# A two-layer graph network: part of the second layer's scatter as rounded part and rest, and the last stage by groups of blocks

## The reference

```
# layer 0
e      = leaky_relu(concat(x[src], x[dst]) @ w) @ a
att    = exp(e) / segment_sum(exp(e), src)[src]
x      = layernorm(x + segment_sum(x[src] * att, dst))
# layer 1, 4 heads of 32 channels
H      = x @ W
s      = leaky_relu(H_s[src] + H_t[dst])          # H_s, H_t: two scores per head and node
s      = exp(s - max(s))
alpha  = s / (segment_sum(s, src) + 1e-8)
agg    = segment_sum(alpha * H[dst], src) + x @ residual_projection
x      = layernorm(x + elu(agg))
```

## Time and profile before

| | |
|---|---|
| the profiled execution's own time | 3574.67 us |
| its span, first to last instruction | 3572.9 us |
| TensorE busy | 3143.2 us, 88% |
| VectorE busy | 3083.1 us, 86% |
| ScalarE busy | 2138.4 us, 60% |
| GpSimd busy | 47.3 us, 1% |
| second layer's scatter, L1243 | 4802 records, first at 2397.6, last at 3473.6 us |
| `exponent`, L1268, mean of 49 | 459 ns |
| last stage, first operation to the end of the span | 3479.4 to 3572.9 us |

### The profile page before, as it was taken

The page is one execution under the profiler, slowest core; times in us unless marked ns, Lnnn a source line. Parts: engine busy times, 40 slices in busy tenths (PEclk is TensorE's granted clock), DMA queues, the critical chain, the costliest instruction groups (busy, mean ns, idle before and its releaser), DMA issues. The chain is left out here.

```text
span 3572.9 us, 97665 instructions
## 1 busy us (share of the span) xinstructions
PE 3143.2 (88%) x40120; PEld 2920.0 (82%) x40120; DVE 3083.1 (86%) x4702; ACT 2138.4 (60%) x4348; POOL 47.3 (1%) x104
## 2 busy tenths in 40 slices
PE   2666669999999999599999999969999999999980
PEld 1666657777777777599999999969999999999980
DVE  5999988899999999899999999968888888888867
ACT  1333338777787777599999999943333333333330
POOL 0000000000000000000000000000000000000000
PEclk9888879999999999799999999989999999999995
DMA  2000012222222222133333333224444444444421
GB/s 54 13 10 12 8 34 87 86 90 86 89 82 91 86 85 81 47 96 97 97 96 97 97 97 97 85 96 149 146 146 147 150 147 149 147 146 149 148 69 36
DMA packets 172961, 332.80 MB, mean 93 GB/s; under 512 B 54673, under 2 KB 108517, under 8 KB 172514
## 3 DMA queue, kind: packets, MB, share of 16 engines
q1 hardware_dynamic: 172514, 326.50, 29.7%
HBM read 320.77 MB, written 5.66 MB: 91 GB/s over the span
## 5 line engine op out<-in xcount | busy, mean ns | idle before, releaser
L1243 PE MATMUL l_acc<-e,l_lane_wide 128*128 128x132 f32 x4802 | 615.2, 280 | 0.0
L1243 PEld LDWEIGHTS l_acc<-e,l_lane_wide 128*128 128x128 f32 x4802 | 566.4, 190 | 0.0
L902 PE MATMUL l_gathered<-xp,l_src_onehot 128*128 128x128 bf16 x7203 | 463.3, 220 | 28.2 <-DVE l_src_onehot L829 28.2
L621 PE MATMUL sc_z<-sc_onehot,pq 128*128 128x256 f32 (+1 forms) x2450 | 427.1, 297 | 43.9 <-DVE sc_leaky L564 42.2
L1174 DVE TENSOR_TENSOR e<-l_gathered,l_weight 128x896 f32<-128x896 f32 x343 | 373.4, 1089 | 102.6 <-PE l_gathered L1230 102.2
L1230 PE MATMUL l_gathered<-hp,l_onehot 128*128 128x128 bf16 x7203 | 458.9, 219 | 0.0
L902 PEld LDWEIGHTS l_gathered<-xp,l_src_onehot 128*128 128x128 bf16 x7203 | 404.8, 98 | 42.8 <-DVE l_src_onehot L829 28.3
L748 DVE TENSOR_TENSOR l_lane<-iota_b,l_lane_pairs 128x896 bf16<-128x896 bf16 x686 | 421.5, 614 | 0.0
L564 DVE SCALAR_TENSOR_TENSOR sc_leaky<-sc_z,sc_leaky 128x1024 f32<-128x1024 f32 (+3 forms) x325 | 369.8, 1138 | 46.0 <-ACT sc_leaky L704 42.8
L1230 PEld LDWEIGHTS l_gathered<-hp,l_onehot 128*128 128x128 bf16 x7203 | 407.3, 98 | 0.1
L704 ACT ACTIVATE sc_leaky<-sc_z 128x1024 f32<-128x1024 f32 (+3 forms) x325 | 309.9, 953 | 154.4 <-PE sc_z L625 95.9
(11 more groups left out here) (208 smaller groups left out, 4944.9 us busy)
## 6 DMA issues: line engine op xcount, KB each, us to landing
l_got<-edge_rows_wide SPq DMA_DIRECT2D x343, 448.0 KB, 3.6
l_got<-edge_rows_src SPq DMA_DIRECT2D x343, 224.0 KB, 3.2
placed<-edge_rows SPq DMA_DIRECT2D x144, 512.0 KB, 3.6
out_dram<-X SPq DMA_DIRECT2D x1, 3072.0 KB
edge_rows<-bin_bytes SPq DMA_DIRECT2D x98, 6.1 KB
edge_rows_wide<-bin_rows SPq DMA_DIRECT2D x98, 12.2 KB
placed<-edge_rows SPq DMA_DIRECT2D x24, 64.0 KB, 2.8
placed<-edge_rows SPq DMA_DIRECT2D x6, 256.0 KB, 3.5
```

What stands on the lines that cost most here:

```text
L621: nc.tensor.matmul(z[:, b, 0:nw, :], PQ[:, b0 + b, q, 0:C], hot[:, r % HOTS, b, 0, 0:nw, :], start=(b == u and q == 0), stop=False)
L902: ins = nc.tensor.matmul(gps[:, t % 2, i * P:(i + 1) * P], hot[:, t % RING, i, :], parts[:, g * GX + i, q, :], start=(q == 0), stop=(q == 2))
L1243: ins = nc.tensor.matmul(acc[:, b % 2, 0:CW], lane_wide[:, t % 2, i, :], msg[:, t % 2, i, :], start=(n == 0), stop=(n == NB - 1))
```

## The change

In `layer1` three of the seven bins (`SPLIT` = 3) are scattered as a rounded part and a rest, side by side in one fp32r matmul of 2 x 132 columns; the rests gather in columns 132 to 263 of the accumulator. The other four go as f32 as before. VectorE weighs six bins, and the seventh is weighed by ScalarE in four activations of 32 channels, one for each head, after its rounding of the three. VectorE's `take_low` is the last of its step; on ScalarE `take_high(t)` and `weigh_last(t)` come first and `exponent`, `copy_weights(t + 1)`, `widen(t + 1)` and `take` behind them. ScalarE's `take` copies the low sums too, and GpSimd adds them to `S` and `den4` and takes one from X (for the ELU).

```
-                        pe.wait_ge(s["messages"], t - 1)
+                        pe.wait_ge(s["last_message"], t - 1)
...
-                    for i in range(GX):
-                        n = g * GX + i
-                        ins = nc.tensor.matmul(acc[:, b % 2, 0:CW], lane_wide[:, t % 2, i, :], msg[:, t % 2, i, :], start=(n == 0),
-                                               stop=(n == NB - 1))
+                    for i in range(SPLIT, GX):
+                        if i == GX - 1:
+                            pe.wait_ge(s["last_message"], t + 1)
+                        nc.tensor.matmul(acc[:, b % 2, 0:CW], lane_wide[:, t % 2, i, :].bitcast(F32), msg[:, t % 2, i, :],
+                                         start=(g == 0 and i == SPLIT), stop=False, skip_group_check=True)
+                    pe.wait_ge(s["low"], t + 1)
+                    for i in range(SPLIT):
+                        last = g == PER - 1 and i == SPLIT - 1
+                        ins = nc.tensor.matmul(acc[:, b % 2, 0:2 * CW], lane_wide[:, t % 2, i, :],
+                                               halves[:, t % 2, i].rearrange("p h c -> p (h c)"), start=False, stop=last,
+                                               skip_group_check=True)
...
+                def take_low(t):
+                    dve.wait_ge(s["high"], t + 1)
+                    nc.vector.tensor_tensor(halves[:, t % 2, :, 1, :], msg[:, t % 2, 0:SPLIT, :], halves[:, t % 2, :, 0, :],
+                                            ALU.subtract).then_inc(s["low"], 1)
...
+                def add_low(b):
+                    pool.wait_ge(s["taken"], b + 1)
+                    nc.gpsimd.tensor_tensor(S[:, b, :], S[:, b, :], lows[:, b % 2, 0:C], ALU.add)
+                    nc.gpsimd.tensor_tensor(den4[:, b, :], den4[:, b, :], lows[:, b % 2, C:CW], ALU.add).then_inc(s["summed"], 1)
...
+                def take_high(t):
+                    act.wait_ge(s["messages"], t + 1)
+                    act.wait_ge(s["weights"], t + 1)
+                    nc.scalar.copy(halves[:, t % 2, :, 0, :], msg[:, t % 2, 0:SPLIT, :]).then_inc(s["high"], 1)
+
+                def weigh_last(t):
+                    b, g = divmod(t, PER)
+                    i, n = GX - 1, g * GX + GX - 1
+                    for e in range(HEADS):
+                        ins = nc.scalar.activation(msg[:, t % 2, i, e * D:(e + 1) * D], gps[:, t % 2, i * P + e * D:i * P + (e + 1) * D],
+                                                   ACT.Copy, scale=weight[:, b % 2, n, e:e + 1])
+                    ins.then_inc(s["last_message"], 1)
```

```
+                def measure(g):
+                    dve.wait_ge(s["added"], g + 1)
+                    for i in range(count(g)):
+                        ins = nc.vector.bn_stats(stats[:, g * PER + i, :], total[:, g % BANKS, i * C:(i + 1) * C])
...
+                for c in (slice(0, 2 * PER), slice(2 * PER, NB)):
+                    ch.link(nc.vector.reciprocal(den4[:, c, :], den4[:, c, :]))
+                    for g in range(c.start // PER, -(-c.stop // PER)):
+                        divide(g)
+                        if g >= 1:
+                            add_residual(g - 1)
+                add_residual(G - 1)
+                for j in range(len(BATCHES)):
+                    for g in range(*BATCHES[j]):
+                        measure(g)
+                        if j >= 1 and g == BATCHES[j][0]:
+                            factors(j - 1)
+                    variance(j)
+                factors(len(BATCHES) - 1)
...
+                def begin(g):
+                    if g >= BANKS:
+                        wait_normed(pe, g - BANKS)
+                    nc.tensor.matmul(total[:, g % BANKS, 0:count(g) * C], k.ident[:], flat(X, g), start=True, stop=False)
+                def add_up(g):
+                    pe.wait_ge(s["positive"], g + 1)
+                    nc.tensor.matmul(total[:, g % BANKS, 0:count(g) * C], k.ident[:], flat(S, g), start=False, stop=False)
+                    pe.wait_ge(s["exponent"], g + 1)
+                    nc.tensor.matmul(total[:, g % BANKS, 0:count(g) * C], k.ident[:], flat(R, g), start=False, stop=True
+                                     ).then_inc(s["added"], 1)
+                for g in range(BANKS):
+                    begin(g)
+                for g in range(G):
+                    add_up(g)
+                    if BANKS <= g + 4 < G:
+                        begin(g + 4)
...
+                for g in range(G + 1):
+                    if g < G:
+                        negative(g)
+                    if g >= 1:
+                        positive(g - 1)
+                        exponent(g - 1)
+                for j in range(len(BATCHES)):
+                    act.wait_ge(s["variance"], j + 1)
+                    nc.scalar.activation(dev[:, batch(j)], squares[:, batch(j)], ACT.Sqrt, scale=1.0 / C, bias=ln_eps[:]
+                                         ).then_inc(s["deviation"], 1)
+                    act.wait_ge(s["factors"], j + 1)
+                    for g in range(*BATCHES[j]):
+                        if g not in BY_VECTOR:
+                            norm(g)
```

More of the change, by code:

```diff
@@ L1103, in layer1 @@
             "chain", "const", "hot", "scored", "read", "top", "all", "negated", "exp", "staged", "lane", "lane_wide", "gathered",
-            "messages", "weights", "added", "taken")}
+            "messages", "last_message", "weights", "high", "low", "added", "taken", "summed")}
         loaded = [ctx.semaphore(f"l1_loaded{h}") for h in range(LOADS)]
@@ L1291, in _ @@
                         stage((t + 4) // PER)
+                    if 0 <= t < R:
+                        take_high(t)
+                        weigh_last(t)
                     if (t + 1) % PER == 0 and 0 <= (t + 1) // PER < NB:
@@ L1917, in _, with add_and_norm @@
                 nc.vector.tensor_tensor(xs[:], X[:], rden[:].unsqueeze(2).to_broadcast([P, NB, C]), ALU.mult)
-def add_and_norm(nc, k, tag, X, S, R, before, out):
+def add_and_norm(nc, k, tag, X, S):
     NB = k.NI
@@ L1925, in add_and_norm @@
         ask = ctx.enter_context(nc.sbuf_tensor(f"{tag}_ask", [P, 1], F32))
-        chain, a_req, a_done, fin, st = (ctx.semaphore(f"{tag}_{n}") for n in (
-            "chain", "act_asked", "act_done", "finished", "stored"))
+        chain, a_req, a_done = (ctx.semaphore(f"{tag}_{n}") for n in (
+            "chain", "act_asked", "act_done"))
         asked = []
@@ L1956, in _, with lower_by_one, elu_and_norm, sb @@
                     emit().then_inc(a_done, 1)
+def lower_by_one(nc, X):
+    with Stage(nc):
+        with nc.Block() as block:
+            @block.vector
+            def _(dve):
+                nc.vector.tensor_scalar(X[:, 0:NBK, :], X[:, 0:NBK, :], -1.0, None, ALU.add)
+def elu_and_norm(nc, k, X, S, R, den4, eps, out):
+    NB, PER, BANKS, N = NBK, 4, 8, out.shape[0]
+    G = -(-NB // PER)
+    BATCHES = ((0, 2), (2, 5), (5, 8), (8, 11), (11, G))
+    BY_VECTOR = (3, 7, 11)
+    with Stage(nc) as ctx:
+        def sb(name, shape, dt=F32):
+            return ctx.enter_context(nc.sbuf_tensor(f"fin_{name}", shape, dt))
+        s = {n: ctx.semaphore("fin_" + n) for n in (
+            "chain", "gap", "decay", "divided", "summed", "negative", "positive", "exponent", "added", "stats", "variance",
+            "deviation", "factors", "normed_act", "normed_dve", "stored")}
+        stats = sb("stats", [P, NB, 6])
+        twice, apart, squares = sb("twice_mean", [P, NB]), sb("apart", [P, NB]), sb("squares", [P, NB])
+        dev, rstd, shift, ln_eps = sb("deviation", [P, NB]), sb("rstd", [P, NB]), sb("shift", [P, NB]), sb("ln_eps", [P, 1])
+        total = ctx.enter_context(nc.psum_tensor("fin_total", [P, BANKS, 512], F32))
+        def blocks(g):
+            return slice(g * PER, min((g + 1) * PER, NB))
+        def count(g):
+            return min(PER, NB - g * PER)
+        def flat(t, g):
+            return t[:, blocks(g), :].rearrange("p b c -> p (b c)")
+        def batch(j):
+            return slice(BATCHES[j][0] * PER, min(BATCHES[j][1] * PER, NB))
+        def wait_normed(eng, g):
+            if g in BY_VECTOR:
+                eng.wait_ge(s["normed_dve"], len([i for i in BY_VECTOR if i <= g]))
+            else:
+                eng.wait_ge(s["normed_act"], g + 1 - len([i for i in BY_VECTOR if i <= g]))
+        with nc.Block() as block:
@@ L1958, in _ @@
             @block.sync
             def _(sp):
[L1960 to L1966, removed]
+                for g in range(G):
+                    wait_normed(sp, g)
+                    rows = slice(g * PER * P, min((g * PER + count(g)) * P, N))
+                    if count(g) * P == rows.stop - rows.start:
+                        sp.dma_start(out[rows].rearrange("(b p) c -> p b c", p=P), X[:, blocks(g), :]).then_inc(s["stored"], 16)
+                    else:
+                        sp.dma_start(out[rows], X[0:rows.stop - rows.start, g * PER, :]).then_inc(s["stored"], 16)
@@ new lines, in _ @@
```

(8 more changed lines are left out.)

112 lines of the change are left out of this document (84 added, 28 removed).

## The result

Four runs of the changed kernel gave a median of 3476.99 us (3475.55 to 3479.29), four of the kernel before 3575.99. The ratio is 0.9724, interval 0.9707 to 0.9741: faster by 99 us, 3480 was forecast. The profiled execution took 3477.6, its span 3475.8.

The account below looks back on a forecast made before the run. TensorE bounded layer 1's loop, VectorE much of the last stage. Gains 59.5 + 2.7 - 1.2 + 35 = 96.0 from 3574.7 gave 3478.7; with the median 1.7 above, 3480 (60%, 3465 to 3495; 8 in 10, 3448 to 3512).

Parts of the forecast that it names:

- 59.5 + 2.7 - 1.2 + 35 = 96.0: Gains in us: layer 1's 334 steps, its last nine steps, minus GpSimd's bare additions at the end, plus the last stage.
- TensorE's step, 2.86: Layer 1: eight f32 records 0.93 and three fp32r ones 0.40 cut TensorE's step by 0.30 to 2.86 us.
- VectorE's step, 2.65 and 2.02: Layer 1: VectorE needs 2.65 us a step, find_top 2.02 more each seventh: 20.64 in seven steps, 2.95 a step.
- The stall, 0.84 in seven steps: Layer 1: TensorE waits for the last message in the step with find_top, making the step 2.98 us.
- rivals B and D: Layer 1: B, late last message, 3.07 a step, 3510, 15%; D, ScalarE's order sets the step, 3.31, 3594, 3%.
- Rival A: Layer 1: VectorE's lateness is absorbed and TensorE alone sets 2.86 a step; 3440, 8%.
- GpSimd beside VectorE: Layer 1: GpSimd pays for contention, 452 ns alone and 597 beside VectorE; VectorE's two-input subtraction kept to 0.69 us.
- Rival E: Layer 1: VectorE stands still while GpSimd works, 61 us on it, of which 50 come through; 3530, 2%.
- The last stage: From 93.5 to 58.5 us, gain 35; TensorE idles behind group 0's norm, which stands behind all ScalarE passes.
- The lower clock: Last stage: after its pause TensorE starts at clock 0.51 for its first 4 us of work, costing 1.75 us.
- ScalarE's twelve norms: Last stage's tail: twelve norms at 0.26 take 3.2 us, with the last batch's root behind them.
- Rival C: Last stage: TensorE stays at 1.2 GHz all through, 15 us more; 3495, 12%.

Follow-up runs that it names:

- last message last: The changed kernel with the seventh bin's matmul moved behind the three fp32r ones in layer 1's scatter: 3468.7 us, ratio 0.9716, step 2.945 us.
- GpSimd free: The changed kernel without GpSimd's addition of the low sums and the one taken from X: 3477.2 us, ratio 0.9724, step 2.972 us.
- after: The changed kernel itself, against the kernel before: 3477.0 us, ratio 0.9724, layer 1 step 2.973 us.
- the later scatter and make before the rest: The changed kernel with scatter one step later on TensorE, three buffers, and VectorE's make ahead of its rest: 3435.8 us, ratio 0.9619, step 2.859 us.
- four bins split: The changed kernel with four of seven bins split instead of three (SPLIT = 4): 3538.8 us, ratio 0.9906, step 3.158 us.

## Why the prediction was right

**The frame.** The sum was 59.5 + 2.7 - 1.2 + 35 = 96.0 from the profiled execution. Alone, layer 1 gave 62.4, where 59.5 + 2.7 - 1.2 = 61.0 were forecast, and the last stage 33.0 where it was 35. The two misses have opposite signs. That the profiled execution came within 1.1 us of the forecast for it (3477.6 against 3478.7) is luck; the terms are good to 1 or 2 us.

**TensorE's step, 2.86.** Measured 2.86. The two terms were off against each other: the f32 records 0.88 instead of 0.93, the three fp32r ones 0.45 instead of 0.40. That was a matter of reading: by their starts has the six f32 records at 0.64 and the four fp32r ones at 0.56, where the prediction gave them 0.68 and 0.52. The 264 columns cost like the 256: records start 0.12 us apart behind a first distance of 0.20, in layer 0 as here. No figure is near the upper bound of 0.233.

**VectorE's step, 2.65 and 2.02.** Measured 2.62 to 2.67 and 2.02. The subtraction took 0.57 and the four activations 0.82, as worked out, which rules out rivals B and D.

**The stall, 0.84 in seven steps.** Measured 0.76, at the place named: the last message, in the step with `find_top`. The step is TensorE's 2.86 and this stall; VectorE's sum lies just below it, at 2.945 where it sets the pace (last message last). The two limits are thus only 0.03 a step apart, some 9 us in all. By the sum alone (2.95) the forecast would have been 3470, inside the range as well, so the total could not have told them apart. The runs do. GpSimd free changed nothing because VectorE is late by the same 2.0 us at each `find_top` as long as it is back on time before it. With the scatter's order changed the step fell with VectorE's work unchanged, but only down to its sum. My expectations for both runs took the sum for the limit in after, against the prediction's own working; the first failed, and the second named the right number with a wrong reason. Rival A (TensorE alone) appears only when both limits are gone, in the kernel with the later scatter and make before the rest.

**GpSimd beside VectorE.** The prediction held that GpSimd alone pays. That was wrong: VectorE's subtraction lengthened from 570 to 687 ns when GpSimd worked beside it (the 48 of 343 that overlap one of GpSimd's additions took 683 to 687, the others 556 to 574), which is what the Trainium skill, GPSIMD Engine Reference, Specifications, says of instructions with two SBUF inputs. It cost nothing, as it fell where VectorE had time (the kernel with GpSimd free). GpSimd paid too: its 128-element addition took 454 ns alone and up to 762 beside VectorE. The evidence in the earlier trace rows did not bear on the question: in the kernel before, 48 of the 49 additions of L890 overlap VectorE's weighing and `make`, and none a subtraction. Rival E was out all the same, as the kernel with GpSimd free shows.

**The last stage.** Counted from 3415.7, the first operation's place if it had stood directly ahead of the second: ScalarE's passes ended at 25.0 (25.6 forecast), TensorE stood from 16.2 to 28.7 (17 to 28.8), took up work at clock 0.50 for some 6 us (4), ended at 48.2 (47.5), the last store went at 55.9 (54), the end came at 60.1 (58.5). Three terms were mis-sized. The lower clock cost more: the first four f32 matmuls of 512 columns took 1.87, 1.71, 1.71 and 1.27 us from start to start, 3.1 us above four times 0.86, where 1.75 had been put in. The columns cost less: 0.86 for 512 is 1.68 ns a column instead of 1.76, 0.8 us less for 9600. ScalarE's twelve norms took 4.13 us until the root behind them (3464.80 to 3468.93), 0.345 apart, instead of 3.2 by L944's 0.26; why is open. Not foreseen: VectorE stood 3.15 us ahead of its second operation for nothing that the profile shows ("issue"). The stage's first operation came 2.3 us after the last copy, before it was 5.3, so the start as a whole cost the same and the stage gained 33.2 from copy to end. The table was loaded once, for 1.28 us, and the root started 0.02 us behind it. The Trainium skill, ScalarE: Activation LUTs, What ACT_TABLE_LOAD costs, has a drain of 1380 ns with a load; none appears here between the last exponential (ends at 3440.72) and the root. Rival C (1.2 GHz throughout) was out: the granted clock was 1.00 from 3452 on, 8 us after TensorE took up work.

Open: why ScalarE's widening takes 959 ns on average in the new loop where it took 935, and why the loop's first weighing comes anywhere from 2389.2 to 2397.6 us, and in the profiled execution with four bins split at 2416.0, in programs that are the same ahead of it. A total of one execution therefore says less on the loop than the step does.

## What to carry to other kernels

Where one engine meets another in short steps and has one long job every few steps, compare two numbers: its sum over the period, and how late the long job makes it against what the other engine tolerates. Either can set the pace, and then work taken off the busiest engine brings nothing (570 against 588 ns, no change) or costs time (3.020 against 2.973). Here a deeper buffer and a later consumer removed the second limit, and only then did shorter work pay: 2.933 by the buffer, 2.859 by both. A third check is the resolution of the measure: counting steps in a stretch was off by up to 0.013 us, half of the 0.03 that one of these readings rests on.

## What the hardware showed that I had not expected

A VectorE subtraction with both inputs in SBUF takes 570 ns by itself and up to 687 beside GpSimd, in this kernel; the first layer's longer one had kept to 691 to 694 in 343 executions although GpSimd worked in that stage too. There the subtraction starts 1 us behind GpSimd's end, so its constant duration proved nothing about contention. After a pause of 12.5 us TensorE worked at a granted clock of 0.50 for some 6 us, after one of 2.8 us for some 3.
